# A new first stage in a decoder layer: gates from a fused weight, DMA transposes, a scan that reads PSUM

## The reference, cut to what is computed

```python
xp = einsum('btd,ed->bte', x, W_in)                       # [2,512,512]
dt = softplus(einsum('btd,hd->bth', xp, W_dt) + b_dt)     # 32 heads
a  = exp(dt[..., None] * -exp(log_A))                     # 32 x 16 = 512 decays
ys = scan over time: s = a * s + xp
x  = layernorm(x + einsum('btd,ed->bte', ys, W_out))
x  = layernorm(x + cross_attention(x, context))           # 16 heads, 8 kv heads
x  = layernorm(x + self_attention_and_moe(x))             # 16 heads; 8 experts, top 2
```

## Time and profile before

| what | value |
|---|---|
| median of three runs | 1615.64 us |
| profiled execution | 1599.96 us, span 1598.0 us |
| busy share of the span | PE 89%, DVE 69%, ACT 43%, POOL 33% |
| mean granted TensorE clock | 0.954 of full speed |
| first matmul of the cross-attention | 113.63 us after the span's start |
| PE busy in the first 113.6 us | 86.07 us |

### The profile page before, as it was taken

One profiled execution on the slowest core, in us unless ns is written; L12 is line 12 of the kernel. 1 busy time (PEld: TensorE's weight loads), 2 busy tenths in 40 slices (PEclk: granted clock), 3 DMA queues, 4 the chain that ended last, 5 costly groups with the idle time before them and its releaser, 6 DMA issues. The chain is left out here.

```text
span 1598.0 us, 25260 instructions
## 1 busy us (share of the span) xinstructions
PE 1429.9 (89%) x8443; PEld 787.0 (49%) x8443; DVE 1096.5 (69%) x2024; ACT 688.5 (43%) x1370; POOL 533.3 (33%) x691
## 2 busy tenths in 40 slices
PE   7878999999999999975789999998649999999992
PEld 4344444444445444432346665665336656666661
DVE  4677777787777878775567777776476565656664
ACT  4724344444343444332255554545335444444520
POOL 0013333334343434344366665744253000000044
PEclk9989999999999999996799999999959999999996
DMA  9105676666667575771102020000146455444543
GB/s 315 48 14 100 119 143 115 138 119 137 140 116 151 105 149 107 129 141 54 67 1 67 1 67 1 26 1 1 37 155 227 170 194 194 160 141 155 185 117 124
DMA packets 322573, 176.94 MB, mean 111 GB/s; under 512 B 270881, under 2 KB 285217, under 8 KB 322497
## 3 DMA queue, kind: packets, MB, share of 16 engines
q1 hardware_dynamic: 318128, 165.52, 40.8%
q0 software_dynamic: 3200, 10.49, 2.1%
q10 hardware_dynamic: 1168, 0.00, 0.0%
HBM read 90.33 MB, written 18.55 MB: 68 GB/s over the span
## 5 line engine op out<-in xcount | busy, mean ns | idle before, releaser
L1023 ACT ACTIVATE xa_SC<-xa_SC,xa_mn 128x1024 f32<-128x1024 f32 x128 | 147.1, 1149 | 211.3 <-DVE xa_mn L1118 211.2
L1105 DVE SCALAR_TENSOR_TENSOR xa_PN<-xa_SC,xa_rs,xa_PN 128x1024 f16<-128x1024 f32 x128 | 190.7, 1490 | 58.8 <-issue 58.1
L915 PE MATMUL xa_psS<-xa_KT,xa_QT 128*128 128x512 f16 x768 | 186.4, 379 | 4.8 <-DVE xa_mn L1118 3.4
L927 PE MATMUL xa_psO<-xa_PT,xa_V 128*128 128x512 f16 x768 | 173.9, 384 | 11.7 <-DMA xa_PT<-xa_PN 11.7
L1118 DVE CUSTOM_DVE_ANT_0 xa_SC<-xa_psS,maskb 128x1024 f32<-128x1024 f32 x128 | 155.4, 1214 | 13.5 <-PE xa_psS L915 8.9
L849 POOL TENSOR_SCALAR xa_rs<-xa_rc,flag 128x1 f32<-128x1 f32 x128 | 33.9, 265 | 388.0 <-DVE xa_rc L1127 388.0
L851 POOL TENSOR_SCALAR xa_PN<-xa_SC,xa_rc,flag 128x1024 f16<-128x1024 f32 x128 | 152.1, 1188 | 0.3 <-issue 0.2
L1521 ACT ACTIVATE sa_SC<-sa_SC,sa_mn 128x128 f32<-128x128 f32 (+3 forms) x128 | 71.9, 562 | 141.5 <-DVE sa_mn L1617 141.5
L927 PEld LDWEIGHTS xa_psO<-xa_PT,xa_V 128*128 128x128 f16 x768 | 75.7, 99 | 105.2 <-issue 16.9
L1994 PE MATMUL rmoe_psY<-W,rmoe_HT 128*128 128x512 f16 (+1 forms) x576 | 126.9, 379 | 0.3 <-DVE rmoe_HT L2089 0.3
L1979 PE MATMUL rmoe_psG<-rmoe_XGT,W 128*128 128x352 f16 x768 | 125.0, 313 | 1.5 <-DVE rmoe_XGT L2062 1.5
(11 more groups left out here) (227 smaller groups left out, 2632.4 us busy)
## 6 DMA issues: line engine op xcount, KB each, us to landing
W13raw<-in_L_ffn_w_dram SPq DMA_DIRECT2D x16, 2048.0 KB, 11.5
W2raw<-in_L_ffn_w_dram SPq DMA_DIRECT2D x8, 2048.0 KB, 8.3
expert_rows_dram<-zeros SPq DMA_DIRECT2D x11, 512.0 KB, 8.8
xa_WPraw<-in_L_xattn_Wq_dram SPq DMA_DIRECT2D x8, 512.0 KB, 4.9
xa_WOraw<-in_L_xattn_Wo_dram SPq DMA_DIRECT2D x8, 512.0 KB, 4.5
sa_WPraw<-in_L_ffn_wq_dram SPq DMA_DIRECT2D x4, 1024.0 KB, 6.1
sa_WOraw<-in_L_ffn_wo_dram SPq DMA_DIRECT2D x4, 1024.0 KB, 5.3
expert_out_dram<-rows SPq DMA_DIRECT2D x16, 256.0 KB, 2.1
```

Of the source, the lines that this page charges most:

```text
L915: last = nc.tensor.matmul(psS[j % 2][:, c:c + cw], QT[b][:, hq, g, t * P:(t + 1) * P], KT[b][:, hk, c:c + cw], start=(q == 0), stop=(q == 2))
L927: last = nc.tensor.matmul(psO[:, c:], V[b][:, hv, blk, :], PT[g % NPT][:, blk, hp, c:], start=(blk + q == 0), stop=(blk == NBLK - 1 and q ...
L1023: nc.scalar.activation(SC[j % 2][:, 0:w], SC[j % 2][:, 0:w], ACT.Exp, bias=mn[:, j % 4:j % 4 + 1], scale=-1.0, accum_out=sm[:, j % 4:j % 4 ...
L1105: nc.vector.scalar_tensor_tensor(out=PN[j % NPN][:, 0:w // P, 1, :], in0=by_block(SC[j % 2], w), scalar=rs[:, j % 4:j % 4 + 1], in1=PN[j % ...
```

## The change

In `phase_ssm`, with H = 32 heads:

- **Gates.** W_dt and W_in are multiplied first (`fused_gate`, 48 matmuls with 32 columns, into `WZ`), and the gate is `WZ` by x: 12 matmuls for a batch with a result of 32x512 (`gate`). The softplus is done on 32x512, once for a batch. A 0/1 matrix `sel` (32x512, built on GpSimd) then spreads each head's step size over its 16 channels: 2 matmuls for each 128x512 block (`spread_steps`). The decay's Exp reads that bank.
- **xp** stays in PSUM: the scan reads it there. The copies of lines 316 and 317 and the subtraction of line 388 are gone. Banks are shared, so a block of the second batch waits for a scan of the first.
- **Transposes.** The second half of x, W_out and the context are split as they lie (ScalarE or GpSimd the high half, GpSimd the low half) and transposed by DMA from SyncE: 4 of 128x1024, 4 of 128x1024 and 16 of 128x512 in float16.
- **Norm.** ScalarE normalizes, with a scale and a shift that GpSimd computes.
- **Moved.** The first weights of the cross-attention are split by GpSimd in this phase (`ready=True` in `attention`). The zeros are written in phase "n2", and phase "n3" waits for them.

The diff, cut to its core:

```diff
+    identF, causal, maskb, flag, ropeC, ropeS, zeros = consts
+    WPraw, WP, wp_arrived = weights
+        XPB = [[bank[m] for m in (0, 1, 2, 3)], [bank[m] for m in (4, 1, 2, 3)]]
+        ZB = [bank[6], bank[5]]
+        OUTB = [bank[m] for m in (0, 5, 6, 7)]
...
@@ sync
             sp.dma_start(mask_in[:], mask...).then_inc(mask_done, 16)
+            for b in range(B):
+                sp.dma_start(ctx_in[b][:], ctxt[b]...).then_inc(c_in[b], 16)
+            for dst, src, arrived in fetch:
+                sp.dma_start(dst, src).then_inc(arrived, 16)
             sp.dma_start(ropeC[:], rope_in[0]).then_inc(tables_in, 16)
             sp.dma_start(ropeS[:], rope_in[1]).then_inc(tables_in, 16)
+            for t in range(TPB):
+                sp.wait_ge(xn_lo, t + 1)
+                sp.dma_start_transpose(out=XT[:, :, :, (TPB + t) * P:(TPB + t + 1) * P]..., in_=XN[:, t]...).then_inc(x1_turned, 16)
+            for m in range(DC):
+                sp.wait_ge(woutN_lo, m + 1)
+                sp.dma_start_transpose(out=woutT[:, :, :, m * P:(m + 1) * P]..., in_=woutN[:, m]...).then_inc(wout_turned, 16)
             for b in range(B):
+                for i in range(8):
+                    if i % 4 == 0:
+                        sp.wait_ge(cn_lo, 2 * b + i // 4 + 1)
+                    sp.dma_start_transpose(out=CT[:, :, :, at:at + P]..., in_=CN[b][:, i]...).then_inc(ctx_turned, 16)
+            sp.wait_ge(ctx_turned, 16 * 8 * B)
-            sp.wait_ge(zeroed, 16 * (E * CAP // (2 * P) + CTL))
             sp.wait_ge(tables_in, 32)
@@ gpsimd: sel, then the low halves of x and W_out, the context, the weights, the rows
+            for t in range(TPB):
+                pool.wait_ge(xn_hi, t + 1)
+                nc.gpsimd.tensor_tensor(XN[:, t, 1, :], X[:, TPB + t, :], XN[:, t, 0, :], ALU.subtract).then_inc(xn_lo, 1)
+            for m in range(DC):
+                pool.wait_ge(woutN_hi, m + 1)
+                nc.gpsimd.tensor_tensor(woutN[:, m, 1, :], wout[:, m, :], woutN[:, m, 0, :], ALU.subtract).then_inc(woutN_lo, 1)
...
+            for b in range(B):
+                pool.wait_ge(c_in[b], 16)
+                for q in range(2):      # 4 rows of 256: 128x1024
+                    nc.gpsimd.tensor_copy(CN[b][:, rows, 0, :], ctx_in[b][:, rows, :]).then_inc(cn_hi, 1)
+                    nc.gpsimd.tensor_tensor(CN[b][:, rows, 1, :], ctx_in[b][:, rows, :], CN[b][:, rows, 0, :], ALU.subtract)...
+            for i in range(NW):         # 3 pieces of 512
+                split_weights(i)
+            for i in range(NT):
+                row_scale(i)            # ve, rstd, shift
@@ tensor
+            for n in range(len(jobs)):          # the 9 first jobs
+                tr_pe(pe, n)
+            project(0, 0)
+            project(0, 1)
+            fused_gate()                        # waits winN_lo
+            project(0, 2)
+            pe.wait_ge(wz_lo, 1)
+            gate(0)
+            project(0, 3)
+            pe.wait_ge(x1_turned, 16 * TPB)
+            project(1, 0)
+            gate(1)
+            spread_steps(0)                     # waits dt_lo; two banks, dec_done
+            project(1, 1)                       # waits scan_done 2
+            project(1, 2)
+            project(1, 3)
+            spread_steps(1)
+            pe.wait_ge(wout_turned, 16 * DC)
+            for i in range(TPB + 1):
+                output(i)                       # i=0: ys_lo 4, dec_done 8; i=4: ys_lo 8
+            norm_pe(pe, 0); norm_pe(pe, 1); output(5); norm_pe(pe, 2); norm_pe(pe, 3); output(6); output(7)
+            for n in range(TPB, NT):
+                norm_pe(pe, n)
@@ scalar
+            for n in range(len(jobs)):
+                tr_act(act, n)
+            nc.scalar.copy(winN[:, 0], win[:]).then_inc(winN_hi, 1)
+            4 x nc.scalar.copy(XN[:, t, 0, :], X[:, TPB + t, :]); WZ high; 4 x woutN high; Exp of logA
+            gate_exp(0); step_high(0); 4 x decay; gate_exp(1); step_high(1); 4 x scan_high; 4 x decay; 4 x scan_high
+            layer_norm and norm_act in turn
@@ vector
+            9 x tr_dve; winN low; WZ low; negA; gate_max(0); maskb; softplus(0); step_low(0); flag; gate_max(1)
+            4 x scan; softplus(1); step_low(1); 4 x scan_low; 4 x scan; 4 x scan_low
+            5 x add; norm_dve 0, 1; add; norm_dve 2, 3; 2 x add; norm_dve 4 to 7
...
@@ phase_norm "n2": fetch=loads + cleared (the 14 transfers of zeros); "n3": landed=[(zeroed, 16 * len(cleared))]
@@ attention "xa": ready=True, no split of the first weights ahead of the first projection
```

More of the change, by code:

```diff
@@ L243, in _, with project @@
+            pool.wait_ge(half_done, 1)
+            pool.wait_ge(wp_arrived, 48)
+            for i in range(NW):
+                split_weights(i)
+            for i in range(NT):
+                row_scale(i)
         @block.tensor
         def _(pe):
-            def project(b):
+            def project(b, m):
+                if b and m:
+                    pe.wait_ge(scan_done, m + 1)
+                for i, (hw, hx) in enumerate(PAIRS):
+                    for k in range(DC):
+                        last = nc.tensor.matmul(XPB[b][m][:, :], winT[:, hw, k, m * P:(m + 1) * P],
+                                                XT[:, hx, k, b * S:(b + 1) * S], start=(i + k == 0),
+                                                stop=(i == 2 and k == DC - 1))
+                last.then_inc(xp_ready, 1)
@@ new lines, in fused_gate, with gate @@
+            def fused_gate():
+                pe.wait_ge(winN_lo, 1)
+                for c in range(DC):
+                    for i, (hw, hd) in enumerate(PAIRS):
+                        for k in range(DC):
+                            last = nc.tensor.matmul(bank[7][:, c * H:(c + 1) * H], winN[:, hw, k, c * P:(c + 1) * P],
+                                                    wdtT[:, hd, k, :], start=(i + k == 0), stop=(i == 2 and k == DC - 1))
+                last.then_inc(wz_ready, 1)
+            def gate(b):
+                for i, (hw, hx) in enumerate(PAIRS):
+                    for k in range(DC):
+                        last = nc.tensor.matmul(ZB[b][0:H, :], WZ[:, hw, k, :], XT[:, hx, k, b * S:(b + 1) * S],
+                                                start=(i + k == 0), stop=(i == 2 and k == DC - 1))
+                last.then_inc(z_ready, 1)
@@ L335, in scan_high, with step_high @@
+            def step_high(b):
+                act.wait_ge(dt_done, b + 1)
+                nc.scalar.copy(dt16[:, 0, b, :], zb[:, b, :]).then_inc(dt_hi, 1)
+            def decay(n):
+                act.wait_ge(spread, n + 1)
+                if n >= DC:
+                    act.wait_ge(scan_done, n - DC + 1)
+                m = n % DC
+                nc.scalar.activation(dec[:, m, :], bank[6 + m % 2][:, :], ACT.Exp, scale=negA[:, m:m + 1]).then_inc(dec_done, 1)
             def scan_high(n):
@@ L355, in _ @@
+            act.wait_ge(wz_ready, 1)
+            nc.scalar.copy(WZ[:, 0], as_dt(bank[7])).then_inc(wz_hi, 1)
+            act.wait_ge(w_in, 48)
+            for m in range(DC):
+                nc.scalar.copy(woutN[:, m, 0, :], wout[:, m, :]).then_inc(woutN_hi, 1)
+            act.wait_ge(small_in, 32)
             nc.scalar.activation(logA[:], logA[:], ACT.Exp).then_inc(expA_done, 1)
+            gate_exp(0)
+            step_high(0)
             act.wait_ge(negA_done, 1)
             for n in range(DC):
-                gate_exp(n)
@@ L637, in head_loads, with attention @@
              Wv[:, bass.ds(kv * HD, HD)].rearrange("(k p) c -> p k c", p=P))]
-def attention(nc, name, X, XT, KVT, identF, weights, Wq, Wk, Wv, Wo, kv_heads, groups, keys, mask_of, flag, rope):
+def attention(nc, name, X, XT, KVT, identF, weights, Wq, Wk, Wv, Wo, kv_heads, groups, keys, mask_of, flag, rope, ready=False):
     NS = groups * TPB
@@ L1047, in half @@
                         piece_high(*piece[:2])
-            act.wait_ge(first_in, 48)
-            for i in range(NWP):
-                piece_high("wp", i)
+            if not ready:
+                act.wait_ge(first_in, 48)
+                for i in range(NWP):
+                    piece_high("wp", i)
             for i in range(JP):
@@ L1135, in half @@
                     jobs(h, b, j, first, last, 1)
-            for i, (dst, src) in enumerate(wp_pieces):
+            for i, (dst, src) in enumerate(wp_pieces if not ready else []):
                 dve.wait_ge(wp_hi, i + 1)
```

386 lines of the change are left out of this document (181 added, 205 removed).

## The result

The changed kernel took 1587.95 us, the median of four runs (1587.12 to 1590.18), beside 1615.04 us for the kernel before on the same chip (1613.34 to 1615.85). The ratio is 0.9837, 95% interval 0.9823 to 0.9851: 27.1 us faster. The forecast was 1591.1 us, 24.5 us faster, with a range of 1584 to 1603. The profiled execution took 1587.12 us, 1585.4 us of it the span.

The account below looks back on a forecast made before the run. Bound: a chain alternating between PE and the ACT/DVE gate chain, no single engine. The new chain's links put cross-attention's first matmul at 89.1 us, not 113.6: 1615.64 - 24.5 = 1591.1 us, range 1584 to 1603.

Parts of the forecast that it names:

- step 6: First batch's spread 0.44, decay 0.7, two scans 2.3, four hand-overs of 0.1: second scan done at 44.5 us.
- Step 2: fused_gate, 48 matmuls with 32 columns after the first two projections: taken as 2.8 us, ending at 23.2.
- step 1: Phase start, first jobs unchanged: project(0,0) starts at 15.13 us, two blocks end at 20.4.
- Step 4: DMA transposes of x, behind the loads, land at 33.8 us; PE, ready at 31.1, waits 2.7.
- Steps 5, 7 and 9: project(1,0) with gate(1), project(1,1) to (1,3), outputs 0 to 4: 5.26, 7.9, 13.2 us, each plus 1.7 for the clock.
- The cover: Moved work stays hidden: GpSimd done near 50 us, context transposes by 75 against 88, zeros in "n2" cost nothing.
- signs of being wrong: PE waiting on x beyond 40, SyncE ending the phase, "n2" +2 us, PSUM scans over 1.3, cross-attention length changing over 3.
- A: Rival: transposes of x come late, at 40 to 45 us; gain 13 to 18, 1598 to 1603 us; chance 0.14.
- E: Rival: clock stays up, transposes of x land before 31.1; gain 30 to 33, 1583 to 1586 us; chance 0.13.
- B: Rival: step-size chain, not PE, sets the phase; output 0 near 65 us, gain 17, 1599 us; chance 0.1.
- C: Rival: DMA transposes cost by instruction or block, deciding from 3.7 us each; at 4.8, 1644 us; chance 0.05.
- GpSimd beside VectorE: First phase: softplus operations and low halves may each wait 1.2 to 2.3 us; sum unchanged, range takes 3 us.

Follow-up runs that it names:

- Run 3: Changed kernel with the four DMA transposes of x issued ahead of the second context half, weights and rope: 1583.16 us, ratio 0.9811 to the kernel before.
- Run 9: Kernel of Run 3 plus a 128x1 Exp on ScalarE ahead of the first decay, to load the table early: 1583.69 us, ratio 0.9809 to the kernel before.
- Run 7: Changed kernel with each of the 16 context transposes issued twice: 1588.6 us, ratio 0.9834 to the kernel before.
- run 4: Changed kernel with the cross-attention's first weights split at that phase's start again, by ScalarE and VectorE: 1590.71 us, ratio 0.9859 to the kernel before.
- Run 1: The kernel before, unchanged, profiled once more: 1611.14 us.
- run 8: Changed kernel with each of the 16 context transposes issued three times: 1603.83 us, ratio 0.9932 to the kernel before.
- runs 2: Changed kernel with GpSimd waiting for each pair of gathers to land before issuing the next: 1588.73 us, ratio 0.9843 to the kernel before.
- run 11: Kernel of Run 3 with one pair of gathers at a time and VectorE's additions spread over the last expert: 1573.49 us, ratio 0.9761 to the kernel before.

## Why the prediction was right

The first matmul of the cross-attention was forecast for 89.1 us and came at 87.54. What each step added to the chain:

| step | forecast, us | measured, us | difference |
|---|---|---|---|
| 4 x1_turned | at 33.8 | at 32.24 | -1.6 |
| 5 project(1,0), gate(1), clock | 5.3 + 1.7 | 6.9 | -0.1 |
| 6 spread, decay, two scans | 3.7 | 5.1 (39.14 to 44.23) | +1.4 |
| 7 project(1,1) to (1,3), clock | 7.9 + 1.7 | 10.2 | +0.6 |
| 8 spread, four decays | 3.2 | 3.4 | +0.2 |
| 9 outputs 0 to 4, clock | 13.2 + 1.7 | 12.95 | -1.9 |
| 10 norms, outputs 5 to 7 | 10.0 | 9.7 | -0.3 |
| 11, 12 tail, barrier | 5.8 + 1.1 | 7.05 | +0.1 |

The differences add up to 1.6 us, the phase's surplus over the forecast. The chain ran as forecast, link by link; what was off were sizes, and in step 6 the assumption that the table load lay beside other work. That the sum held to 1.6 us is in part luck: 2.3 us of terms too small stand against 3.9 too large. One slip in the working costs nothing: by its own numbers gate(0) ends at 28.5, not at 28.7.

**Step 2** was off by half and cost nothing. 48 matmuls with 32 columns took 1.35 us, 28 ns each, where 2.8 were taken. The nearest row, 128 columns, has 2.84; the text gave its whole price to the weight loads, and only the lower bound of 0.7 went by columns. With step 1, which came 0.8 us early (14.37 for 15.13), TensorE reached the wait for x at 28.9 and not at 31.1. As x came 1.6 early too, these 2.2 us became a longer wait, 3.34 for 2.7. A term ahead of a wait on another resource is not in the sum.

**Step 4** named the right thing, transposes behind the loads, and put them 1.6 us too late. The issues began at 21.04 and not at 23.7, took 2.3 us each and not 1.2 to 1.9, and the last landed 2.1 us after its issue and not 0.5. Run 3 shows that it was a matter of the queue's order: 9.13 us of issue for four became 6.01, and the wait went away with the slow clock behind it, 4.8 us together.

**Step 6** said that the table load was hidden, as ScalarE would be idle. It was idle, but the load came only after the first spread, so the 1.28 us stood in the chain. It is no rule that a load waits for its instruction's operand: the table for the second batch was loaded at 50.84 in after, 4.2 us before its decay, and ahead of the spread that feeds it (54.44). In run 3 (ScalarE) it went the same way:

```profile
45.31 1.28 ACT L401 ACT_TABLE_LOAD   x1
...
50.31 2.65 ACT L401 ACTIVATE dec<-bank,negA 128x512 f32<-128x512 f32 x4 [3.72 <-PE bank L330]
```

The decays of the second batch wait for two semaphores (spread and scan), those of the first for one. Whether that makes the difference no run shows. Run 9 adds a second limit that takes over once x comes earlier: VectorE's other work.

**Steps 5, 7 and 9** charged 1.7 us three times for the clock. Measured are 1.5 (4.27 for 2.76), 2.2 (10.28 for three times 2.69) and nothing: 58 to 71 us had a granted clock of 1.00. The third, 1.7 us, is the largest miss of the sum. The clock fell behind idles of 3.34 and 1.69 us, and the third charge stood behind one of 0.87. That isn't a rule either: in run 9 the same idle of 0.87 was followed by 0.79 from 52 to 60 us, and the five outputs took 14.80 us. Behind the phase nothing had been charged, and cross-attention's first 24 matmuls took 8.20 us, against 6.70 in the earlier trace rows. The two go together in most runs and not in all: with 14.80 for the outputs (7 and 9) these 24 took 6.63 and 6.83, with 13.11 they took 8.15 to 8.23 in six kernels, but 6.73 in run 3 and 7.07 in run 4.

**From the profile to the median.** The text took the gain over to the median, 15.7 us above the profiled execution, and gave no reason for these 15.7. Run 1 gives it for 11 to 12 of them: the execution that was read lacked the hole. It lies far behind the changed phase and both kernels have it, so the gain is not touched. The two profiled executions that have it, run 1's 1611.14 and after's 1587.12, differ by 24.0, and the medians by 27.1, with an interval of 24.1 to 28.6 by the ratio. That 26.1 in the phase became 27.1 in the medians is thus no confirmation to the microsecond. Where the profile sets in varies too. The first projection starts between 15.1 and 15.9 us in the kernels with before's first phase and between 13.7 and 14.8 in the others, so some 0.8 us of the phase's 26.1 may be chance.

**The cover** was right, with numbers. GpSimd was done at 47 (forecast 50), the context's transposes were issued by 57.6 (by 75), the zeros in "n2" by 734.9, 4.4 us ahead of the phase's last instruction. The signs of being wrong stayed away: "n2" kept its length, the scans from PSUM took 1.14 us each (1.14 from SBUF in the earlier trace rows), and the cross-attention grew by 1.3 us, under the 3 named. Run 7 doubled the transposes for nothing, run 8 found the end of the cover.

**The rivals.** A (x later than 33.8) did not occur, nor did E's 30 us or more, nor did B: spread(1) found its step sizes at 54.44 without a wait. C has the right mechanism, a cost per instruction, at 1.27 to 2.3 us and not the 3.7 at which it decides; 24 took 36.4 us of SyncE's issue. For the context the text had 0.6 us of data and at most 1.9 of issue each; it was the issue, 1.36. The Trainium skill, "VectorE: DVE Perf Modes", section The three transpose paths, has 1309 ns for one 128x128 block. The trace has about that time, but for an instruction of four blocks (1.27, run 8) or eight (1.37, W_out), and 1.9 for sixteen. So here it reads as a price per instruction that grows little with its blocks. Going by blocks, an estimated 168 us, would have been wrong by a factor of 4.6.

**GpSimd beside VectorE.** Line 464 took 1.61 us beside GpSimd's subtraction of line 264, and 0.68 for the second batch with GpSimd idle (47.41 us), and GpSimd's four subtractions of line 249 took 6.08 where the four of W_out took 4.49, since the first stood beside VectorE's 2.29 us (line 500). By the rule of "SBUF — State Buffer" in the Trainium skill, section Who interferes with whom, the two exclude each other, and the rows agree. It cost nothing that ended last, as forecast.

## What to carry to other kernels

Walk a change along its chain of waits and keep the term for each link apart: here errors of +1.4 and -1.9 us were inside a sum that held to 1.6, partly by luck, and another of 1.4 vanished in a wait on something else. Look for what stood still in one execution and not in the other before a sum is taken over from a profile to a median: a second profile of the same kernel showed 11.3 us in a part that the change had not touched. And where transfers are moved off an engine, order them by who waits first, and pace those that nobody waits for: the order of one queue was worth 4.8 us and the wait between pairs of gathers 9.7.

## What the runs showed of the hardware that was not expected

- Beside sixteen gathers by GpSimd without a pause, some 200 GB/s for 20 us, TensorE did 4 matmuls in 5 us where it does 35, and the expert took 10.7 to 12.0 us longer, in eleven of twelve profiled executions. At 101 and 105 GB/s (runs 2 and 11) it did not happen. TensorE's idle is marked "issue", so it waited for nothing that the profile shows, and in after its matmuls start at steps of 0.71 us or a multiple. The page of after lists a queue of instructions on the same DMA engines (packets, MB, share):

```profile
q8 instruction: 36, 0.59, 0.2%
```

  So late instructions are a candidate. The queues of instructions in after have no packet from 1500 to 1522 us and the next at 1524.8, behind the gathers; in run 11 one came at 1509, and in before one at 1528, beside the gathers. But in run 1 one came at 1527 too, and its hole opened ten us later. So the packets speak neither for it nor against it; no run took it apart, and one execution of the kernel before had the same gathers and no hole. The Trainium skill, "Runtime: NRT & Kernel Launch", section Instruction fetch mechanics, has instructions fetched by DMA in blocks of 16 KiB, at a cost "mostly hidden"; the 36 packets of this queue have that size, and whether the hole is such a fetch stays open.
- A DMA transpose costs its queue 1.27 us of issue for 128x512 in float16 (run 8) and 1.37 for 128x1024 (W_out in after) when no loads are ahead of it. Behind the loads 128x1024 costs 2.3 (x in after) or 2.1 (W_out in run 3).
- A table load on ScalarE (1.28 us) can wait through 7.16 us of idle time, or run 4.2 us ahead of the instruction that needs it, both in after.
- 48 matmuls with 32 columns and new weights each time ran at 28 ns each (1.35 us), against 59 with 128 columns (2.84).
